# Layer 3 attention: the banks of the mirrored scores, the place of the turning, and the order of a tile's transfers

## The reference

```python
def _L3_xattn_ref(q, k, v, gamma):
    N_HEAD = 8
    B, Dq, Lq = q.shape
    Dv, Lk = (v.shape[-2], v.shape[-1])
    ...
    qh = q.reshape(B, h, dq, Lq)
    kh = k.reshape(B, h, dq, Lk)
    vh = v.reshape(B, h, dv, Lk)
    scale = 1.0 / jnp.sqrt(jnp.asarray(dq, dtype=q.dtype))
    qk = jnp.einsum('bhdq,bhdl->bhql', qh, kh) * scale
    sm = jax.nn.softmax(qk, axis=-1)
    ret = jnp.einsum('bhql,bhdl->bhdq', sm, vh)
    ret = ret.reshape(B, Dv, Lq)
    return gamma * ret
...
x = x + _L3_xattn_ref(_layernorm(x, axis=-1), ctx_2048, ctx_2048, L3_xattn_gamma)
```

## Time and profile before

| | us |
|---|---|
| median of 3 runs | 2195.09 (2190.27 to 2209.36) |
| the profiled execution's own time | 2198.6 |
| its span | 2196.7 |
| `maxima` L2885, 512 times | 320.0 busy |
| `exponent` L2857, 512 times | 281.1 busy |
| `turned_pair` L2785, 1024 matmuls | 130.7 busy |
| `read` L2800, 2048 matmuls | 165.4 busy |
| first mirrored score to last readout copy | 1441.9 to 1842.4 |

### The profile page before, as it was taken

How to read it: one execution, slowest core, us unless ns; L and a number is a source line. 1 busy time by engine, 2 the same in 40 slices (tenths; PEclk the granted TensorE clock), 3 DMA queues, 4 the chain that set the end, 5 groups by cost and what they waited for, 6 DMA issues and landing times. The chain is left out here.

```text
span 2196.7 us, 43555 instructions
## 1 busy us (share of the span) xinstructions
PE 1792.4 (82%) x14590; PEld 1354.6 (62%) x14590; DVE 1553.8 (71%) x3825; ACT 987.5 (45%) x2422; POOL 894.9 (41%) x1043
## 2 busy tenths in 40 slices
PE   6989845299796788889898899778888885989993
PEld 5879612187565677777776788644444442557772
DVE  7975731277759688988988666689888993554446
ACT  3743231034233445545554333257777775523330
POOL 3410016434248466666666510014334333643331
PEclk9989956599999799999999899979999998989996
DMA  7821036520213000000000311037767762433337
GB/s 225 294 81 56 10 107 177 150 77 6 70 46 114 1 0 0 0 0 0 0 0 0 59 30 31 1 65 142 143 142 144 145 131 86 124 109 99 107 105 244
DMA packets 150753, 182.46 MB, mean 83 GB/s; under 512 B 40193, under 2 KB 132593, under 8 KB 146481
## 3 DMA queue, kind: packets, MB, share of 16 engines
q1 hardware_dynamic: 140769, 158.05, 27.7%
q0 software_dynamic: 9808, 22.23, 3.4%
HBM read 121.78 MB, written 56.79 MB: 81 GB/s over the span
## 5 line engine op out<-in xcount | busy, mean ns | idle before, releaser
L2885 DVE TENSOR_REDUCE mx<-bank 128x2 f32<-128x512 f32 x512 | 320.0, 679 | 41.4 <-PE bank L2763 39.5
L2857 ACT ACTIVATE e<-bank 128x512 f32<-128x512 f32 x512 | 281.1, 595 | 99.4 <-PE bank L2785 92.6
L1914 POOL TENSOR_TENSOR q_l<-q_l,rot_l 64x512 f32<-64x512 f32 x128 | 162.4, 1268 | 130.9 <-DVE rot_l L2112 130.9
L2785 PEld LDWEIGHTS bank<-q,k 64*128 64x128 f32 x1024 | 79.1, 188 | 163.8 <-ACT e L2857 113.2
L2785 PE MATMUL bank<-q,k 64*128 64x256 f32 x1024 | 130.7, 333 | 57.7 <-ACT e L2857 41.8
L2800 PE MATMUL bank<-e,val 128*32 128x256 f32 x2048 | 165.4, 395 | 0.7 <-ACT e L2857 0.6
L1946 PE MATMUL bank<-qcT,wq_abs 96*128 96x128 f32 x1024 | 127.4, 285 | 0.0
L1946 PEld LDWEIGHTS bank<-qcT,wq_abs 96*128 96x128 f32 x1024 | 121.5, 198 | 2.5
L2763 PE MATMUL bank<-k,q 62*128 62x256 f32 x1024 | 111.7, 296 | 13.0 <-DVE mx L2885 9.0
L3072 POOL DMA_INDIRECT y<-y,y_row x71 | 69.2, 975 | 126.7 <-DVE y L3347 121.9
L1971 PE MATMUL bank<-wvo,rd_l 128*128 128x256 f32 x512 | 116.4, 381 | 0.0
(11 more groups left out here) (445 smaller groups left out, 4685.9 us busy)
## 6 DMA issues: line engine op xcount, KB each, us to landing
k<-k_parts SPq DMA_DIRECT2D x128, 128.0 KB, 5.1
q<-q_parts SPq DMA_DIRECT2D x64, 256.0 KB, 4.1
got<-rows SPq DMA_DIRECT2D x71, 129.0 KB, 2.1
k_parts<-k_parts_a SPq DMA_DIRECT2D x64, 128.0 KB, 3.1
moe_rows<-zero_a SPq DMA_DIRECT2D x16, 512.0 KB
w<-in_e0w SPq DMA_DIRECT2D x16, 512.0 KB, 3.6
q_parts<-parts SPq DMA_DIRECT2D x64, 128.0 KB, 2.5
rec<-rec_rows SPq DMA_DIRECT2D x64, 128.0 KB, 2.5
```

The source lines that it names most:

```text
L1914: nc.gpsimd.tensor_tensor(q[64:P, j, four(m), :], q[64:P, j, four(m), :], rot[64:P, j, four(m), :], ALU.add).then_inc(s["rope_added"], 1)
L2785: last = nc.tensor.matmul(scoresT(r)[:, lt * D:(lt + 1) * D], k[used, b, at + lt * P:at + lt * P + P], q[used, b, at:at + D], start=True, ...
L2857: nc.scalar.activation(e[:, slot(i, r), :, :].rearrange("p k n -> p (k n)"), scoresT(r)[:, :], ACT.Exp).then_inc(s["exp_ready"], 1)
L2885: v.tensor_reduce(mx[:, a.n, r % 2, 0, at:at + 2], scores(r)[:, :].rearrange("p (a n) -> p a n", a=2), AX.X, ALU.max, negate=True).then_in ...
```

## The change

The mirrored scores of unit n of a tile go into bank (4, 5, 7)[n mod 3] instead of a bank fixed by `r`. So each unit from 3 on waits for the exponent three units back; the first three of a tile wait for 1, 4 and 4 back. The turning moves from before quad 2 to the second pair of quad 1, between its score pair and its readout half, and waits for unit 5 instead of unit 6. PE's wait for the copied rows moves from the second to the first pair of quad 2. ACT copies the rows after unit 6 instead of after unit 7. In SP's tile the rows come first, and the gather comes before the inverse load.

```diff
-        turned_bank, turned_after = (4, 5, 7, 4), (1, 4, 4, 3)
-        scoresT = lambda r: c.bank[turned_bank[r]]
+        turned_banks = (4, 5, 7)
+        scoresT = lambda i, r: c.bank[turned_banks[(4 * i + r) % 3]]
+        turned_after = lambda i, r: 3 if 4 * i + r >= 3 else (1, 4, 4)[r]
...
             def tile(a):
+                if a.exists(1):
+                    lay_rows(a.to(1))
                 if a.exists(-2):
                     store_inverse(a.to(-2))
-                if a.exists(1):
-                    lay_rows(a.to(1))
                 if a.exists(AHEAD):
                     store(a.to(AHEAD))
+                if a.exists(-1):
+                    gather(a.to(-1))
                 if a.exists(-2):
                     load_inverse(a.to(-2))
-                if a.exists(-1):
-                    gather(a.to(-1))
...
-                pe.wait_ge(s["exp_ready"], max(unit_ready(a.t, i, r) - turned_after[r] for r in (2 * p, 2 * p + 1)))
+                pe.wait_ge(s["exp_ready"], max(unit_ready(a.t, i, r) - turned_after(i, r) for r in (2 * p, 2 * p + 1)))
...
-                        last = nc.tensor.matmul(scoresT(r)[:, lt * D:(lt + 1) * D], k[used, b, at + lt * P:at + lt * P + P],
+                        last = nc.tensor.matmul(scoresT(i, r)[:, lt * D:(lt + 1) * D], k[used, b, at + lt * P:at + lt * P + P],
...
             def tile(a):
                 for i in range(QU):
-                    turning = i == 2 and a.exists(1)
-                    if turning:
-                        turn_max(a.to(1), unit_ready(a.t, 1, 2))
                     for p in range(2):
-                        if turning and p == 1:
+                        if (i, p) == (2, 0) and a.exists(1):
                             pe.wait_ge(s["rows_ready"], tile_ready(a.t + 1))
                         turned_pair(a, i, p)
                         if a.exists(LEAD):
                             score_pair(a.to(LEAD), i, p)
+                        if (i, p) == (1, 1) and a.exists(1):
+                            turn_max(a.to(1), unit_ready(a.t, 1, 1))
...
             def tile(a):
                 for i in range(QU):
-                    if i == 2 and a.exists(1):
-                        rows_copy(a.to(1))
                     for r in range(4):
                         exponent(a, i, r)
+                        if (i, r) == (1, 2) and a.exists(1):
+                            rows_copy(a.to(1))
```

More of the change, by code:

```diff
@@ L2856, in exponent @@
                 act.wait_ge(s["used_ready"], quad_ready(a.t, i) - 2)
-                nc.scalar.activation(e[:, slot(i, r), :, :].rearrange("p k n -> p (k n)"), scoresT(r)[:, :],
+                nc.scalar.activation(e[:, slot(i, r), :, :].rearrange("p k n -> p (k n)"), scoresT(i, r)[:, :],
                                      ACT.Exp).then_inc(s["exp_ready"], 1)
```

## The result

Over 20 runs of each kernel, side by side, the changed kernel takes 2187.78 us and the kernel before 2201.84 us (medians). The ratio is 0.9935, 95% interval [0.9918, 0.9953]: 14 us faster, where 24 were forecast, and short of the 1% that I had set as the bound of what can be told with few runs. One run of the changed kernel (7252.68 us) and one of experiment 3 (3466.32 us) lie far from all others and are in no ratio.

A forecast was written before the change was run, and what follows sets the result against it. The PE/ACT loop and SP's issuing were taken to share the bound. Tiles go from 12.44 to SP's 11.7 us: 20 us over 27 tiles plus 3.5 outside, 23.5 less, giving 2171 us, range 2158 to 2190.

The forecast's parts named there:

- the SP term of the sum: SP's loop per tile: 11.23 us of issuing plus 0.45 of waiting at the store, 11.7, taken as the tile time.
- SP's floor: SP's issuing per tile, six steps keeping their instructions: stays 11.23 us, summed from each start to the next.
- The PE term: PE's loop per tile gets 0.71 us shorter, 12.06 to 11.35: 0.31 at the turning, 0.39 at quad 3.
- the gain of quad 1 is nothing: Quad 1 could start at 2.49, but its second pair stays at 4.15, its exponent standing behind the readout copy.
- what SP's lateness adds: The old tile's 12.44 us read as the PE loop's 12.06 plus an addition from SP being late.
- The inverse's landing: SP's wait before load_inverse for the stored inverse to land: from 1.1 us to about 0, bounds 0 and 0.9.
- POOL's parts: SP's wait at store for POOL's x_low, after losing cover: 0.45 us a tile, bounds 0 and 1.2.
- the likely heir of the gain: Rival, chance 0.27: the wait moves from inverse to store; 12.1 to 12.4 us a tile, 2182 to 2190 us.
- A shifted loop is not a shorter one: SP's order: issuing rows 1.47 us earlier, ahead of the inverse store, alone gives nothing where SP sets the pace.
- DVE: 10.98 us of work fits in 11.35; more x_done waits, up to 0.8 a tile, charged nothing (0.2 without slack).
- clock rival: Rival, chance 0.05: PE slots at 1.2 GHz take 2.16 instead of 1.24 us; a quarter of tiles so, 2213 us.
- The tail: The last four tiles, outside the 27 intervals, gain 0.71 us each by the PE loop; with tile 0, 3.5.

The follow-up runs named there:

- experiment 3: Changed kernel with DVE's statistics of x moved from unit (1, 3) to unit (3, 1): ratio 0.9934 to the kernel before.
- Experiment 8: Changed kernel with POOL issuing the query parts, statistics at unit (3, 1), and the inverse load inside the block of loads: ratio 1.0377 to the kernel before.
- experiment 4: Changed kernel with the inverse store again ahead of the rows in SP's tile, gather still ahead of the inverse load: ratios 0.9898 and 0.9912 to the kernel before.
- experiment 5: Kernel before with only the gather moved ahead of the inverse load: ratio 0.9961 to the kernel before.
- experiment 7: POOL instead of SP issues the query parts: changed kernel 0.9916; inverse store first 0.9886; also statistics later 0.9888; old banks, inverse first, gather ahead 0.9992.
- experiment 6: Changed kernel with one more 8 KB DMA per tile on SP's queue: 0.9999; with one 128 KB load less in tiles 4 to 31: 0.9911 to the kernel before.
- late statistics: DVE's statistics of x moved to unit (3, 1), here on the changed kernel with POOL issuing the parts and inverse store first: 0.9888 to the kernel before.

## Why the prediction was wrong in size

The direction, the place and the limit (SP) were right. The failed step is the SP term of the sum, "SP loop 11.23 + 0.45 = 11.7": it measured 12.06, 11.96 and 11.95. What it left out is 0.46 us a tile of drawn-out issues (below, SP's floor). The PE term failed the other way. Point by point:

**PE loop: 11.35 forecast, 11.02 measured.** Of the 0.33, 0.10 are quad 1: "the gain of quad 1 is nothing" was a misreading of the earlier trace rows. The exponent at 1749.16 followed the readout copy, so I took it to wait for it. It waited for its own pair, 1748.62 + 0.54 = 1749.16. In the changed kernel the next exponent starts 0.46 after the copy (1468.84 to 1469.30), and the second pair of quad 1 comes at 4.05, not 4.15. Another 0.19 are the turning: from the second pair of quad 1 to quad 2 pass 1.48 (4.05 to 5.53), which is 0.24 more than the 1.24 of other slots, where I had charged 0.39 and a slot of 1.28. Since SP set the pace, this miss cost the sum nothing.

**SP's floor: 11.23 is not what it needs.** That was a sum of starts to starts in a tile in which little stood in the way. In the changed kernel the same sum is 1.58 + 1.40 + 1.32 + 3.94 from the tile shown above, and for the two steps that are delayed there 1.46 + 1.39 from this one, 11.09 in all:
```profile
1609.05 1.33 SPq L2633 DMA_DIRECT2D den<-nd  x2
1610.51 1.21 SPq L2652 DMA_DIRECT2D rec<-rec_rows  x2
1611.90 0.83 SPq L2606 DMA_DIRECT2D q<-q_parts  x1
```
SP's waits in the last 25 of the 27 tiles, changed kernel:
```profile
SPq L86 <- DMA rec_rows<-inv: 9.0, 14, 1.2
SPq L86 <- ACT rows L2840: 3.0, 2, 2.1
SPq L86 <- POOL parts L2723: 2.7, 6, 0.8
```
and kernel before:
```profile
SPq L86 <- DMA rec_rows<-inv: 16.9, 18, 1.4
SPq L86 <- DVE inv L2893: 2.6, 3, 1.2
```
These tiles have a mean of 12.14 in the changed kernel, of which 0.59 are waits. Less 11.09, 0.46 is left that no wait explains (0.45 and 0.58 in the other profiles). SP's timeline says what it is: now and then one issue takes far longer than the others in the same place of SP's order, as this pair of 2.43 (1.21 in a clean tile).
```profile
1634.54 2.43 SPq L2652 DMA_DIRECT2D rec<-rec_rows  x2
```
In these 25 tiles 13 of 425 issues are over 0.2 longer than the shortest of their place, the worst by 1.2. Summed over the 17 places, mean less shortest is 0.50 a tile (0.38 of it in these 13), while the pauses between issues exceed their shortest by 0.70, of which the waits are 0.59. The kernel before held the same: 12.47, less 11.23, less 0.78 of waits, leaves 0.46, with 0.58 of drawn-out issues. I had booked that remainder as "what SP's lateness adds" and not as SP's own work, and so let it vanish. It is the miss: with 0.46 more, my SP loop is 12.14 instead of 11.7, and the same sum gives 12 us of gain (27 x 0.3 + 3.5) instead of 23.5.

**The inverse's landing: 0 forecast, bounds 0 and 0.9.** Measured are 0.36 a tile here, 0.43 and 0.24 in the other two profiles. The 1.5 us of the rows between loads and inverse store did not work like the 1.0 us of pause in the earlier trace rows, which was one tile. From the inverse store to the inverse load pass 4.2 where nothing is waited for (4.38 in my sum) and up to 5.4 where the landing is. Perhaps it is because the rows are traffic themselves; no run shows that.

**POOL's parts: 0.45 forecast, 0.11 measured** (0.02 and 0.09 in the other profiles). The inverse mostly landed early enough: from the inverse load at 1610.51 POOL's product starts 3.80 later, `x_low` ends at 8.56, and SP reaches the store at 8.65, drawn-out issues included (8.32 in my sum). These last two errors, 0.36 too low and 0.34 too high, cancel in the sum, by luck. Calling the wait at `store` the likely heir of the gain was wrong all the same: the time came out next to that rival's 13 to 5 us less, but without its mechanism. Experiment 8 shows that the chain is there; in the changed kernel it has slack.

**A shifted loop is not a shorter one** held: in experiments 4 and 5 rows first gives no gain. The Trainium skill's page DMA: Bandwidth & Descriptors (Queues, rings and completion order) says that each DMA engine consumes its descriptors in ring order; by that the rows would not overtake the loads, and the ratios agree with it.

**DVE** was charged at nothing, and experiment 3 shows that to be right, with 31.1 us of visible waiting up to the last readout copy.

**The clock.** PE waits longer for rows in total (33.0 us instead of 28.9), and behind some of these waits the granted clock falls to 1.2 GHz:
```profile
1732.91 0.80 PE L2786 MATMUL bank<-q,k 64*128 64x256 f32 x4 [2.12 <-DMA q<-rows]
...
1734.07 1.08 PE L2801 MATMUL bank<-e,val 128*32 128x256 f32 x8
1735.07 0.79 PE L2786 MATMUL bank<-q,k 64*128 64x256 f32 x4
```
Slots of 2.16 again, as in the earlier trace rows; from 1733 to 1739 the granted clock is 0.50. I count 5 turned pairs so drawn out in the 27 tiles here, 2 and 1 in the other two profiles, 3 before, 9 with the banks alone and none with the order alone. At 0.92 each, the banks alone gave back some 8 us that way. They come one to three in a row, 0.9 to 2.8 us; the prediction's clock rival had 5 us a tile, a figure for which it showed no row. That rival, clock losses from cycling through banks among them, did not come true: where SP has room (experiment 7) the granted clock is 1.00 with the old banks and 0.99 to 1.00 with the rotated ones. The Trainium skill's page TensorE: Matmul & The Clock Gate (A second HAM failure mode: psum-queue depth-cycling), which the prediction cites there, tells of one such kernel and not of several. In the profiles before, after and with the banks alone each fall follows a wait of PE for the rows, of 1.6 to 2.8 us; not each such wait is followed by one (2.4 us with the banks alone). In experiments 4, 6 and 7 some falls follow a wait of 1.4 to 1.5 us for DVE's maxima instead.

**The tail.** Four last intervals: 42.9 instead of 45.0, 2.1 less for 2.8 forecast.

Open is what draws out SP's issues for 0.46 us a tile, and why the inverse store first shows more in the runs than in its first profile. Neither was tried further. The fastest that I ran are the changed kernel with POOL's parts and the inverse store first, with or without late statistics (0.9886 and 0.9888). Without POOL's DMAs it is experiment 4's swap of two lines.

## What to carry to other kernels

Where an in-order queue sets the pace, take its cycle as the mean over many rounds, pauses included, and not as the sum of issues in one clean round. The remainder (0.46 us a tile here, before and after) is the queue's own time and will still be there. Shortening an engine's loop behind such a queue buys nothing by itself (0.9995 here), and reordering buys only the waits that other issues now cover. The longest new wait in a profile can be free: move it out of the way and see, before pricing it.

## What the runs showed of the hardware that I had not expected

Once POOL issues DMAs of its own, the end of the stage takes 4 us longer (17.2 to 18.2 against 13.3 to 15.5, and 17.2 against 13.3 with the old banks). About one of SP's DMA issues in thirty takes 0.2 to 1.2 us longer than the same issue in other tiles, 0.4 us a tile in all (13 of 425 in the changed kernel), with no semaphore wait behind it; what causes it was not tried. One DMA of 8 KB more per tile on SP's queue, whose data nobody reads and on which no engine was seen to wait, costs 0.3 to 0.4 us a tile, and takes the ratio from 0.9935 to 0.9999.
